# Step sizes of a selective scan: bias row inside the matmul, delta assembled straight from PSUM

## What is computed

```
x_dbl = einsum('bkdl,kcd->bkcl', xs, x_proj_w)
dts, Bs, Cs = split(x_dbl, [R, R + N], axis=2)      # R = 24, N = 16
dts = einsum('bkrl,kdr->bkdl', dts, dt_projs_w)
dts = softplus(dts + dt_projs_b[None, :, :, None])
...
h = h * exp(dts * A) + dts * u * B
```

## Time and profile before

| | us |
|---|---|
| median of 3 runs (2244.14 to 2249.29) | 2245.13 |
| profiled execution: span from the first to the last instruction | 2244.7 |
| VectorE busy in the span | 1575.2 (70%) |
| TensorE busy | 1984.1 (88%) |
| ScalarE busy | 1144.9 (51%) |
| GpSimd busy | 1297.0 (58%) |

### The profile page before, as it was taken

One profiled execution on the slowest core, in us unless ns is written; L12 is line 12 of the kernel. 1 busy time (PEld: TensorE's weight loads), 2 busy tenths in 40 slices (PEclk: granted clock), 3 DMA queues, 4 the chain that ended last, 5 costly groups with the idle time before them and its releaser, 6 DMA issues.

```text
span 2244.7 us, 20167 instructions
## 1 busy us (share of the span) xinstructions
PE 1984.1 (88%) x5826; PEld 919.6 (41%) x5830; DVE 1575.2 (70%) x1505; ACT 1144.9 (51%) x1258; POOL 1297.0 (58%) x464
## 2 busy tenths in 40 slices
PE   7988588888888888888888888989995999999997
PEld 3332133333333333333333333456653555555554
DVE  6978999999999999999999999774553000000000
ACT  4788666666776676776767666211213112122111
POOL 0110499999999999999999999401233011111110
PEclk9987599999999999999999999999997999999999
DMA  6448622233222233222232220611226233333300
GB/s 193 151 175 280 212 75 75 70 98 79 84 66 65 75 100 91 65 75 75 61 105 67 77 73 19 229 42 57 85 85 223 85 119 124 123 119 126 126 24 7
DMA packets 82402, 229.13 MB, mean 102 GB/s; under 512 B 14031, under 2 KB 40257, under 8 KB 80816
## 3 DMA queue, kind: packets, MB, share of 16 engines
q1 hardware_dynamic: 76208, 211.54, 29.6%
q0 software_dynamic: 6144, 16.98, 2.1%
HBM read 166.39 MB, written 64.03 MB: 103 GB/s over the span
## 4 chain that ended last, share of the span: by engine, by line
PE 46%; DVE 23%; issue 17%; POOL 8%; ACT 3%; DMA 1%; DVEq 0%; SPq 0%; ACTq 0%; POOLq 0%
DVE arena L1705 15%; PE ps L1489 11%; PE ps L1502 11%; PE ps L1229 6%; POOL arena L604 4%; POOL arena L587 4%; PE ps L1439 3%; PE ps L1213 2%; PE ps L1110 2%; DVE ps L1688 1%; PE ps L1226 1%; PE ps L1139 1%; PE ps L1390 1%; PE ps L1428 1%; DVE arena L1572 1%
## 5 line engine op out<-in xcount | busy, mean ns | idle before, releaser
L604 POOL TENSOR_TENSOR arena<-arena 128x2048 f32<-128x2048 f32 x192 | 868.3, 4533 | 16.6 <-DVE arena L1705 15.7
L1229 PE MATMUL ps<-arena 128*128 128x512 f32 x1536 | 727.7, 596 | 27.7 <-POOL arena L604 27.6
L1705 DVE TENSOR_TENSOR_SCAN arena<-arena,ps 128x1024 f32<-128x1024 f32 x264 | 587.5, 2266 | 0.0
L880 ACT ACTIVATE arena<-ps 128x1024 f32<-128x1024 f32 x384 | 390.7, 1017 | 248.0 <-PE ps L1213 246.1
L1213 PE MATMUL ps<-arena 96*128 (+1 forms) x1296 | 366.7, 384 | 129.3 <-DVE arena L1705 112.7
L1229 PEld LDWEIGHTS ps<-arena 128*128 128x128 f32 x1536 | 288.4, 190 | 287.7 <-issue 194.0
L587 POOL TENSOR_TENSOR arena<-arena 128x1024 f32<-128x1024 f32 x120 | 283.1, 2359 | 103.5 <-DMA arena<-b_rows 103.5
L2066 DVE TENSOR_TENSOR arena<-ps,arena 128x384 f32<-128x384 f32 x32 | 17.8, 557 | 450.4 <-PE ps L1502 450.4
L1688 DVE TENSOR_TENSOR ps<-ps,arena 128x1024 f32<-128x1024 f32 x264 | 309.1, 1216 | 12.6 <-PE ps L1213 12.6
L873 ACT ACTIVATE arena<-arena 128x1024 f32<-128x1024 f32 x264 | 300.8, 1139 | 8.9 <-DVE arena L1705 8.3
L1213 PEld LDWEIGHTS ps<-arena 96*128 96x128 bf16 x1296 | 112.9, 98 | 461.3 <-DVE arena L1705 215.7
(11 more groups left out here) (225 smaller groups left out, 1611.9 us busy)
## 6 DMA issues: line engine op xcount, KB each, us to landing
arena<-b_rows SPq DMA_DIRECT2D x240, 256.0 KB, 4.2
arena<-in_w SPq DMA_DIRECT2D x16, 2304.0 KB, 13.3
delta<-arena SPq DMA_DIRECT2D x24, 512.0 KB, 2.9
delta_x<-arena SPq DMA_DIRECT2D x24, 512.0 KB, 3.1
arena<-delta SPq DMA_DIRECT2D x24, 512.0 KB, 3.6
arena<-delta_x SPq DMA_DIRECT2D x24, 512.0 KB, 4.6
slot_in<-arena SPq DMA_DIRECT2D x8, 772.0 KB, 8.1
arena<-slot_in SPq DMA_DIRECT2D x8, 772.0 KB, 18.0
```

The lines of the kernel that those rows point to most:

```text
L604: nc.gpsimd.tensor_tensor(hst[:, h:h + 2], hst[:, h:h + 2], c_sb[:, c:c + 2], ALU.mult).then_inc(p2_ok, 2)
L880: nc.scalar.activation(c_sb[:, u % RING], C_PS, ACT.Copy).then_inc(c_free, 1)
L1229: mm = pe.matmul(Y_PS[:, h * 512:(h + 1) * 512], ident, hst[:, u % HRING, h * 512:(h + 1) * 512], start=False, stop=(u == UN - 1))
L1705: nc.vector.tensor_tensor_scan(h, f, x, 0.0, ALU.mult, ALU.add).then_inc(sc_ok, 1)
```

## The change

The bias of the step product moves into the matmul: the contraction grows from 48 to 49 rows, the 49th row of the weights holds the bias and the 49th row of `rows` holds ones (the copy out of PSUM adds a column that is one at rows 48 and 112 and zero elsewhere). The bias rows are loaded by two transposing DMAs of their own, between the constants and `xproj_w`.

ScalarE then reads the product once, for |v|; the plain copy of v is gone. max(v, 0) + ln is taken by VectorE from PSUM (`whole_delta`), and it is this instruction that frees the PSUM pair. ScalarE makes 1 + e for every half, and VectorE for none. The order inside a step changes on both engines: ScalarE does |v| of s, then the logarithm of s - 1, then the exponential and 1 + e of s; VectorE does `whole_delta(s - 1)`, `lost_part(s)`, `finish(s - 1)`.

```diff
+            for lo in (DR, H2 + DR):
+                sp.dma_start(dt_w[lo:lo + 1], a["dt_bias"].rearrange("p q r one -> one q r p"),
+                             allow_slow_non_contiguous=True).then_inc(lb_ok, 16)
...
-                nc.scalar.activation(rows[0:H2 + DR, o], fill_slot("xd", p, o)[0:H2 + DR], ACT.Copy).then_inc(rows_ok, 1)
+                nc.scalar.activation(rows[0:H2 + DRB, o], fill_slot("xd", p, o)[0:H2 + DRB], ACT.Identity,
+                                     bias=one_row[0:H2 + DRB]).then_inc(rows_ok, 1)
...
-            def dt_out(p, i):
+            def absolute(p, i):
...
-                nc.scalar.activation(u_mk[:, m % MADE], DT_PS[m % 2], ACT.Abs, bias=bias).then_inc(ab_ok, 1)
-                nc.scalar.activation(d_mk[:, m % MADE], DT_PS[m % 2], ACT.Identity, bias=bias).then_inc(dtev_ok, 1)
+                nc.scalar.activation(u_mk[:, m % MADE], DT_PS[m % 2], ACT.Abs).then_inc(ab_ok, 1)
...
                     if s < HALVES:
-                        dt_out(p, s)
-                        exp_abs(p, s)
-                        if s % J == 0:
-                            one_more(p, s)
+                        absolute(p, s)
                     if s >= 1:
                         log_w(p, s - 1)
+                    if s < HALVES:
+                        exp_abs(p, s)
+                        one_more(p, s)
...
                 if m >= 2:
-                    pe.wait_ge(dtev_ok, m - 1)
+                    pe.wait_ge(pd_ok, m - 1)
+                elif m == 0:
+                    pe.wait_ge(lb_ok, 32)
...
-            pe.wait_ge(dtev_ok, NP * HALVES)
+            pe.wait_ge(pd_ok, NP * HALVES)
...
-                if i % J:
...
-                    chain.link(nc.vector.tensor_scalar(w, u, 1.0, None, ALU.add))
-                else:
-                    dve.wait_ge(w_ok, m // J + 1)
+                dve.wait_ge(w_ok, m + 1)
...
+            def whole_delta(p, i):
+
+                m = p * HALVES + i
+                dve.wait_ge(ln_ok, m + 1)
+                nc.vector.scalar_tensor_tensor(out=d_mk[:, m % MADE], in0=DT_PS[m % 2], scalar=0.0, in1=w_mk[:, m % 2],
+                                               op0=ALU.max, op1=ALU.add).then_inc(pd_ok, 1)
...
-                dve.wait_ge(ln_ok, m + 1)
-                nc.vector.scalar_tensor_tensor(out=d, in0=d, scalar=0.0, in1=w_mk[:, m % 2],
-                                               op0=ALU.max, op1=ALU.add).then_inc(pd_ok, 1)
...
+                    if s >= 1:
+                        whole_delta(p, s - 1)
                     if s < HALVES:
                         lost_part(p, s)
```

More of the change, by code:

```diff
@@ L25 @@
 DR = 2 * R
+DRB = DR + 1
 SR = 2 * N
@@ L182, in hybrid_block_kernel @@
         a_neg = always.take(OJ, 2, N)
-        dt_bias = always.take(OJ, 2, 1)
+        one_row = always.take(1)
         d_sum = always.take(OJ, 1)
@@ L324, in hybrid_block_kernel @@
         ab_ok, u_ok, w_ok, pd_ok = sem("abs_ready"), sem("u_ready"), sem("w_ready"), sem("delta_uncorrected")
-        dtev_ok, lost_ok, ln_ok = (sem(n) for n in ("dt_evacuated", "lost_part", "ln_ready"))
+        lost_ok, ln_ok, lb_ok = (sem(n) for n in ("lost_part", "ln_ready", "ld_bias_rows"))
         xd_ok, xa_ok = sem("dt_rows_filled"), sem("bc_rows_filled")
@@ L363, in hybrid_block_kernel @@
         CONSTS = [
-            (ident, "ident"), (ones, "ones"), (a_neg, "a_logs"), (dt_bias, "dt_bias"), (d_two, "ds"),
+            (ident, "ident"), (ones, "ones"), (a_neg, "a_logs"), (d_two, "ds"),
             (conv_b, "conv_b"), (norm_g, "norm_g"), (norm_b, "norm_b"),
@@ L756, in split_lo @@
                 nc.scalar.activation(parts[:, o, 2], fill_slot("xa", p, o), ACT.Copy).then_inc(lo_ok, 1)
-            def dt_out(p, i):
-                k, j, q, dr = half_of(p, i)
+            def absolute(p, i):
                 m = p * HALVES + i
-                bias = dt_bias[:, q % OJ, dr, :]
                 act.wait_ge(dt_ok, m + 1)
@@ L764, in dt_out @@
                     act.wait_ge(dm_st[m % MADE], m // MADE * 32)
+                elif m == 0:
+                    act.wait_ge(xc_ok, J)
                 elif m == BLANK_FROM:
                     act.wait_ge(zero_st, 16 * E)
-                nc.scalar.activation(u_mk[:, m % MADE], DT_PS[m % 2], ACT.Abs, bias=bias).then_inc(ab_ok, 1)
-                nc.scalar.activation(d_mk[:, m % MADE], DT_PS[m % 2], ACT.Identity, bias=bias).then_inc(dtev_ok, 1)
+                nc.scalar.activation(u_mk[:, m % MADE], DT_PS[m % 2], ACT.Abs).then_inc(ab_ok, 1)
             def exp_abs(p, i):
@@ L777, in one_more @@
                 act.wait_ge(u_ok, m + 1)
-                if m:
+                if m >= 2:
                     act.wait_ge(pd_ok, m - 1)
-                else:
-                    act.wait_ge(xc_ok, J)
                 nc.scalar.activation(w_mk[:, m % 2], u_mk[:, m % MADE], ACT.Identity, bias=ones[:, 0:1]).then_inc(w_ok, 1)
@@ L1164, in delta_product @@
                 if m >= 2:
-                    pe.wait_ge(dtev_ok, m - 1)
+                    pe.wait_ge(pd_ok, m - 1)
+                elif m == 0:
+                    pe.wait_ge(lb_ok, 32)
                 for h in range(2):
-                    mm = pe.matmul(DT_PS[m % 2][:, h * 512:(h + 1) * 512], dt_w[lo:lo + DR, q % OJ, dr],
-                                   rows[lo:lo + DR, k % 2, h * 512:(h + 1) * 512], start=True, stop=True)
+                    mm = pe.matmul(DT_PS[m % 2][:, h * 512:(h + 1) * 512], dt_w[lo:lo + DRB, q % OJ, dr],
+                                   rows[lo:lo + DRB, k % 2, h * 512:(h + 1) * 512], start=True, stop=True)
                 mm.then_inc(dt_ok, 1)
@@ L1611, in lost_part @@
                 u, w = u_mk[:, m % MADE], w_mk[:, m % 2]
-                if i % J:
[L1613 to L1617, removed]
-                    chain.link(nc.vector.tensor_scalar(w, u, 1.0, None, ALU.add))
-                else:
-                    dve.wait_ge(w_ok, m // J + 1)
-                nc.vector.scalar_tensor_tensor(out=u, in0=w, scalar=-1.0, in1=u, op0=ALU.add, op1=ALU.subtract).then_inc(lost_ok, 1)
+                dve.wait_ge(w_ok, m + 1)
+                nc.vector.scalar_tensor_tensor(out=u, in0=w, scalar=-1.0, in1=u, op0=ALU.add, op1=ALU.subtract).then_inc(lost_ok, 1)
+            def whole_delta(p, i):
[3 more added lines that the diff above has]
+                                               op0=ALU.max, op1=ALU.add).then_inc(pd_ok, 1)
             def finish(p, i):
@@ L1653, in _ @@
             nc.vector.tensor_scalar(minus, ident, -1.0, None, ALU.mult)
+            nc.vector.tensor_tensor(one_row, ident[:, DR:DR + 1], ident[:, H2 + DR:H2 + DRB], ALU.add)
             nc.vector.tensor_tensor(d_sum.rearrange("p q one -> p (q one)"), d_two[:, 0], d_two[:, 1], ALU.add).then_inc(setup, 1)
```

## The result

The changed kernel took 2295.69 us (median; 2293.88 to 2296.42), the kernel before 2245.08 on the same chip: a ratio of 1.0221, 95% interval 1.0207 to 1.0236. The forecast was 2293.0. The profiled execution's span went from 2244.7 to 2294.6 us, 49.9 more. The direction, the mechanism and the size were right; one term that the forecast set to nothing was not nothing, and the others' errors cancelled it.

A forecast was written before the change was run, and what follows sets the result against it. VectorE was taken to pace the halves at 6.1 us; after, 23 intervals sum to 191.7 us against 140.5, from an earlier start, so the last `whole_delta` comes 48.3 later: 2244.7 + 48.3 = 2293.0 us, range 2262 to 2312.

The forecast's parts named there:

- VectorE paces the kernel before: Delta stage: VectorE sets 23 intervals of 6.1 us; the 11 us saved on it turn into idle time.
- before, that was covered: Steps with an `x_proj` or `conv` block: before, the block hid because product s + 2 was not yet wanted.
- The ring: Delta stage, once per half: `whole_delta(s - 1)`, product s + 1, |v| of s + 1, logarithm of s, `whole_delta(s)`; 78 in 100.
- One turn: One half of delta: 7.3 us at the half clock, 5.4 at the full, including 1.28 for VectorE's PSUM pass.
- Which clock: TensorE where only products stand: half clock, 3.75 us a product.
- The rival with the full clock: Delta stage: TensorE's clock comes up, last `whole_delta` only 11.8 us later, 2256.5 us; 10 in 100.
- Intervals: Between `whole_delta` starts: seven plain 7.3, seven with ScalarE's split-copy take 9.4, six with block 8.2, one both, two short; 191.7 us.
- The first `whole_delta`: Start of the delta stage: it starts at 106.4 us instead of 109.32, as |v| of half 1 starts at 104.37.
- The bias loads at nothing: Load queue ahead of `xproj_w`: one-element bias runs cost nothing, as a landing until 39.4 us is free.
- the rival: Front of the kernel: the bias load holds the constants up, up to 48 us on top, 2341; 5 in 100.
- a third of the engines: Bias loads: spread over only a third of the sixteen DMA engines, they would still land at about 41 us.
- the prediction's lower bound: Bias loads: 3,072 runs as fast as `xproj_w`'s, 866 packets a microsecond, 3.5 us, landing at 34.5, nothing lost.

The follow-up runs named there:

- e5: Changed kernel with direction rows, step weights and bias row rounded to bfloat16 for the product; 2254.25 us in one run.
- e2: Changed kernel with a second ScalarE read of the product freeing the PSUM pair, as before the change; 2247.76 us, ratio 1.0011.
- e3: Changed kernel with every step product made twice into the same place; 2358.37 us in one run.
- e4: Changed kernel with ScalarE taking the logarithm of half s - 1 ahead of |v| of half s; 2281.32 us, ratio 1.0155.
- e7: Changed kernel with ScalarE's and VectorE's lists back in the order of before, `whole_delta` still freeing the pair; 2332.35 us in one run.
- e1: Changed kernel with the bias loads placed behind `xproj_w`; 2293.03 us, ratio 1.0206 to the kernel before.
- e6: Kernel before with the multiplication by x moved from VectorE to GpSimd, second pair's column copies behind its first seven; 2259.05 us, ratio 1.0063.
- e8: Bias row alone, loads behind `xproj_w`; pair's release, split of 1 + e and both orders as in the kernel before; 2243.39 us, ratio 0.9994.
- e9: Changed kernel with ScalarE's second read freeing the pair, bias loads behind `xproj_w`, 1 + e on VectorE in 14 steps; 2242.35 us, ratio 0.9988.

## Why the prediction was right, step by step

- **VectorE paces the kernel before; the change saves work there that turns into idle time.** The second half is right: busy 121.03 to 112.97 us, idle time before L1617 and L1623 76.5 us (forecast over 60). The first half is right for part of the stage only. In the kernel before, the chain of waits of the first 33 us (108.7 to 142.3) stands on TensorE, on the products and blocks of the earlier trace rows, and after that much of it on VectorE; two of these turns take 8.12 and 8.57 us before and 8.12 and 8.18 after. So the prediction's "before, that was covered" fails for the blocks that stand in a row; the length that it gave such a turn, 8.2, holds. e5 shows VectorE's pace in the changed kernel: with a product of 1.01 us its passes follow without a gap in two of the last four plain turns.
- **The ring.** Right, in its members and in their order (the chain of waits), and shown by four runs that each changed one member: the release (e2, 45.1 of 47.82 us gone), the product's length (e3, 3.41 more in each turn; e5, 38.35 less in all), the order on ScalarE (e4 shorter, e7 longer).
- **One turn.** 7.16 us at the half clock against 7.3. The 0.06 us for reading PSUM was not there: L1623 takes 1.224 us, the same sum from SBUF 1.218. The 1.281 us of L1601 is no sign of PSUM's cost, since taps with only SBUF inputs take as long (1.285); the group of 90 to 303 us, changed kernel:

```profile
L1590 DVE SCALAR_TENSOR_TENSOR arena<-arena 128x1024 f32<-128x1024 f32 x13 | 16.7, 1285 | 0.5
```

- **Which clock.** Right where only products stand: 3.75 us each in the second pair's last steps; TensorE in order of time, changed kernel:

```profile
273.62 3.75 PE L1171 MATMUL ps<-arena 49*128 49x512 f32 x4 [3.41 <-DVE arena L1623]
280.78 3.75 PE L1171 MATMUL ps<-arena 49*128 49x512 f32 x4 [3.41 <-DVE arena L1623]
```

  The rival with the full clock is out for these turns, by e3 as well. Right behind a block the same product takes 1.98 us (forecast 1.85); TensorE in order of time, changed kernel:

```profile
132.00 1.98 PE L1171 MATMUL ps<-arena 49*128 49x512 f32 x4
```

- **Intervals.** 188.30 us against 191.7. Seven plain ones 51.07 (51.1; this match is luck in part, as five are 7.15 to 7.16, one soon after a block 6.66 and the one at the change of the pairs 8.63), seven with a take 63.3 (65.8; 9.04 each, not 9.4), six with a block and the SiLU break 52.9 (54.2), one of both 9.73 (10.8), two short ones 11.34 (9.8): there VectorE waits 0.90 us for 1 + e, which the forecast left out.
- **The first `whole_delta`** 11 us behind the first |v|: right (11.02).
- **The bias loads at nothing**: the mis-sized term. They cost 4.7 us: the constants behind them in the queue arrived at 45.19 instead of by the 39.4 up to which the prediction took it to be free. The sign that it named for this, VectorE idle ahead of L1650, is there with 7.12 us; the rival had 5 in 100. Nothing was also not what its own figures gave, since 41 for a third of the engines lies past 39.4. The limit was too early, too: in e5 the load landed at 41.25 and the first |v| started at 95.05, as early as before (95.37). With landings from 43.73 to 45.19 (the changed kernel, e2, e3, e4, e7) it started at 99.25 to 101.56, and with no wait for the load (before, e1, e6, e8, e9) at 94.83 to 97.16. SyncE's issues, changed kernel:

```profile
20.58 6.27 SPq L394 DMA_DIRECT2D arena<-in_dt_bias  x2
26.90 13.28 SPq L398 DMA_DIRECT2D arena<-in_xproj_w  x4
```

`xproj_w` starts to be issued at 26.90 instead of 21.55 and takes 13.28 us instead of 6.46. The DMA view of the changed kernel, three stretches (26 to 27, 30 to 31 and 34 to 36 us):

```profile
DMA packets 1063, 0.02 MB, mean 17 GB/s; under 512 B 1061, under 2 KB 1061, under 8 KB 1063
```

```profile
DMA packets 434, 0.00 MB, mean 2 GB/s; under 512 B 434, under 2 KB 434, under 8 KB 434
```

```profile
DMA packets 67, 0.02 MB, mean 8 GB/s; under 512 B 67, under 2 KB 67, under 8 KB 67
```

At first the one-element runs go as fast as the nearest row said (866 in a microsecond), and then, from 27 to 31 us, at 191 to 434: the prediction's lower bound, that price for all 3,072, was too low. They are not the whole of it. From 34 to 36 us, at 8 GB/s, a packet holds some 240 bytes, so these are `xproj_w`'s own runs, and only 67 of them move in 2 us; why that load is slow behind the one-element runs stays open. e1 undoes the delay at the front, by 5.13 us; how much of that reaches the end is not settled, as its median is 2.7 lower.

The sum: 48.3 forecast, + 4.7 for the load, - 3.4 for the intervals, + 0.3 behind the stage, 49.9 measured. The forecast's 2293.0 is nearer to 2295.69 than its terms deserve.

## What to carry to other kernels

When an operation is merged away, look at what its completion released. Here a copy of some 1 us on ScalarE freed a PSUM pair early; without it the buffer is free only at the end of the chain that the next buffer's reader stands in, and two buffers work as one. Price the longest circle through all engines' lists (release, refill, read, whatever stands in order behind it) before counting the work saved, and put loads with one-element runs behind every load that someone waits for.

## What the hardware showed that was not expected

- The wait for the load behind the one-element runs differs from one profiled execution to the next, while the loads ahead of it are the same: 7.12 us in the changed kernel, 6.84 in e2, 4.94 in e3, 6.74 in e4, 3.93 in e5, 7.54 in e7.
- Products of 49 rows kept TensorE busy for 21.48 of 30.41 us (e3) at a clock of 0.50 throughout, while a block with 128 rows, behind a like stretch of products and takes, ran at a mean of 0.88 (126 us in the changed kernel) and of 0.69 (e1).
- GpSimd and VectorE did not work side by side on local memory: VectorE passes of 0.69 and 1.22 us took 2.69 and 3.24 next to a GpSimd multiplication, and the multiplication next to the second took 2.66 instead of 2.34 (e6).
